# Second edge stage of a graph network: maps turned edge-major, selections moved to ScalarE, values weighted on VectorE

## The chip, the cores and the metric

The kernel runs as one program on one core of a Trainium2 chip. The metric is the device time of one execution in microseconds (us), the median over the executions shown. The engines of the core are TensorE (matrix products, "PE" in the rows, its weight loads "PEld"), VectorE ("DVE"), ScalarE ("ACT"), GpSimd ("POOL") and SyncE ("SP"), which only issues transfers.

## The reference, cut to what matters

Two message-passing layers over a graph of 12,500 nodes and 200,000 edges, sorted by destination. The change touches the edge part of the second layer:

```python
ms = src_s[edge_src] + dst_s[edge_dst]            # 64 scalars per edge
mv = src_v[edge_src] + dst_v[edge_dst]            # 32 vectors of 3 components
o0a = w1 * ms
o0b = w4 * (einsum('eud,ed->eu', mv, Y1) / SQ3)   # Y1: the edge's direction
o1a = (w2 * ms)[:, :, None] * Y1[:, None, :]
o1b = w3[:, :, None] * mv
o1c = w5[:, :, None] * (cross(mv, Y1[:, None, :]) / SQ2)
ls, lv = eq_lin(concat[o0a, o0b], concat[o1a, o1b, o1c], lin_ws, lin_bs, lin_wv)
a = einsum('ehk,hk->eh', smooth_leaky(alpha), alpha_dot)   # 8 heads, alpha = ls[:, :64]
a = exp(a - segment_max(a)); a = a / segment_sum(a)
ns, nv = segment_sum(vs * a), segment_sum(vv * a)          # per destination node
```

## The kernel before, in words

Edges are cut into 1568 tiles of 128 (`ET`, `R`). A step handles four tiles (`GT = 4`), a pass is eight steps (`STEPS = 8`), and the stage `layer1_edges` is 49 passes (`PASSES`). Each engine has its own program: a body of eight unrolled steps, in which `r` is the step in the pass. The first pass and the last are written out, those between are a loop. Order across engines is kept by counting semaphores. Each engine executes in order, so a wait holds all that is queued behind it. `gate` is a wait on a semaphore that has long been set.

The step `i` of the engines, as far as the change touches it:

- SyncE: `load_windows(i+4)` loads for each tile the window of up to 128 destination rows of the table `TD` (`win`, four slots), from starting rows that it reads into registers. Then follow index and weight loads and `store(i, 6)`, which waits for the totals of step `i-6`.
- GpSimd: gathers with indirect transfers, one per tile, the source rows from `TS` and adds them into `m_` (L1952), as soon as ScalarE has put the destination part there. Then `weighted(i, 8)` (L1936) multiplies the 20 values of each head of step `i-8` by the head's exponential.
- VectorE: `sums(i+1)` makes the products with the direction (`prod`), the two halves of the cross product (`cA`, `cB`, L1981 to L1984, each in two pieces as the components wrap around) and their sum and difference; in every fourth step `scans`; `selections(i+4)` (L1970) compares a row of destination ranks with the partition number, which gives the 0/1 matrix `pick`; `results(i-1)` makes logits and values; `weigh(i+1)` multiplies by the edge weights into `d`; `members(i)` (L2018) makes the 0/1 matrix `q` that sums edges per destination.
- TensorE: `spread_out(i+3)` in two halves (L2138) multiplies `pick` with the windows; `turn_back(i-1)` in two halves (L2187) transposes the mapped results to edge-major; `weights(i+1)` (L2124); `turn(i, 0..2)` (L2149) transposes `d`; `totals(i)` in two halves (L2163) sums the values of step `i-6`; `map_scalars(i)` (L2170) and `map_vectors(i)` (L2176, L2177) apply the linear maps with the weights stationary and 512 edges moving, so that the result has channels on partitions; `logits_up` and `tops_down` (L2196, L2201) transpose logits and segment maxima once per four steps.
- ScalarE: copies out of the PSUM banks: `keep_far` (L2266), `keep(i, 0..4)` (L2275), `keep_totals` (L2286), in `results` the hyperbolic tangent and the scalar values (L2295, L2299), and once per four steps `weigh_up` (L2252), the exponential of the logits.

Transposes, windows and maps take turns in PSUM banks 2 and 3, seven uses per step (`bank`). A matrix product in 32-bit floats stands in the trace as two passes, a transpose as one.

## Time and profile before

| | us |
|---|---|
| median of 3 executions | 9799.34 |
| lowest, highest | 9798.74, 9811.15 |
| profiled execution | 9813.87 |
| its span in the trace | 9812.0 |
| TensorE, VectorE, GpSimd, ScalarE busy | 8373.1, 7735.9, 7372.6, 4874.4 |
| second edge stage, first to last gather | 5335.6 to 9015.3 |

The profiled execution is one execution with the recorder on. Its time is 14.5 us above the median. Busy times are means over stages with different limits, so the stage of the change is read by itself. In a timeline row the first number is the start, in us from the span's start, and the second the busy time; a bracket holds the idle time before it and what ended it.

### The profile page before, as it was taken

To read this page: it belongs to the slowest core of one execution; us is meant where nothing else is said; L and a number is where in the kernel's file an instruction comes from. 1 tells how busy PE (TensorE), PEld (TensorE's weight loads), DVE (VectorE), ACT (ScalarE), POOL (GpSimd) and SP (SyncE) were. 2 spreads that over 40 slices of the span, in tenths; PEclk is the share of its full clock that TensorE was granted. 3 is DMA by queue.
4 is the path that set the end of the run, shared out by engine and by line. 5 is a ranking of instruction groups with operands and counts; after the bars stand their busy time and mean duration, and the time that the engine had idled before them with its cause. 6 is when DMAs were issued, how large, how long until landed. Compare 5 with 4: busy or idle time off the path is not lost. (4 is left out here: it accounts for less than half of the span.)

```text
span 9812.0 us, 193495 instructions
## 1 busy us (share of the span) xinstructions
PE 8373.1 (85%) x35878; PEld 5079.2 (52%) x35878; DVE 7735.9 (79%) x14864; ACT 4874.4 (50%) x9073; POOL 7372.6 (75%) x4571
## 2 busy tenths in 40 slices
PE   0788888888888869999985999999999999998588
PEld 0444444444444422222222777777777777777233
DVE  3177777777777768888886999999999999998465
ACT  0176666666666631121121555555555555555355
POOL 4378888888888878778774888888888888886331
PEclk9599999999999989999997999999999999999799
DMA  5578888888888877778773666666666666665222
GB/s 208 180 161 167 167 168 166 167 167 167 167 167 167 167 213 275 267 271 282 264 270 109 136 137 144 137 143 137 144 138 144 138 142 137 144 137 122 59 70 52
DMA packets 1235170, 1618.04 MB, mean 165 GB/s; under 512 B 222610, under 2 KB 1010589, under 8 KB 1178973
## 3 DMA queue, kind: packets, MB, share of 16 engines
q1 hardware_dynamic: 758950, 1273.86, 40.0%
q0 software_dynamic: 475584, 338.58, 27.1%
q14 instruction: 589, 4.83, 0.2%
q8 instruction: 47, 0.77, 0.0%
HBM read 1533.79 MB, written 444.07 MB: 202 GB/s over the span
## 5 line engine op out<-in xcount | busy, mean ns | idle before, releaser
L1952 POOL DMA_INDIRECT e_m<-TS,e_at x1568 | 2631.8, 1678 | 583.7 <-issue 461.4
L442 POOL DMA_INDIRECT sums<-e_total,e_place x1568 | 2506.9, 1599 | 565.9 <-DMA sums<-e_total,e_place 314.5
L579 PE MATMUL ps<-e_win,e_pick 128*128 128x448 f32 x3136 | 1325.8, 568 | 165.0 <-DVE e_u L476 97.0
L579 PEld LDWEIGHTS ps<-e_win,e_pick 128*128 128x128 f32 x3136 | 612.5, 201 | 921.6 <-issue 864.1
L2275 ACT ACTIVATE e_dT<-ps 128x512 f32<-128x512 f32 x1176 | 660.0, 596 | 495.5 <-PE ps L2149 340.1
L2275 ACT ACTIVATE e_oT<-ps 128x512 f32<-128x512 f32 x784 | 468.9, 598 | 615.1 <-PE ps L2177 373.2
L742 DVE SCALAR_TENSOR_TENSOR r_y<-ps,w_rb,r_rstd 128x512 f32<-128x512 f32 x394 | 295.6, 750 | 579.9 <-issue 533.2
L1096 POOL TENSOR_TENSOR n_zv<-n_zv,n_ast 128x1536 f32<-128x1536 f32 x200 | 703.6, 3518 | 36.6 <-DMA n_zv<-in_x_groups 22.5
L1936 POOL TENSOR_TENSOR e_val<-e_val 128x640 f32<-128x640 f32 x392 | 670.9, 1712 | 61.9 <-ACT e_val L2252 61.9
L2018 DVE TENSOR_TENSOR e_q<-e_row,dstI 128x512 f32<-128x512 int32 x392 | 704.2, 1796 | 13.3 <-PE ps L2163 13.3
L711 PE MATMUL ps<-r_sq,w_avg 128*128 128x512 f32 x788 | 458.1, 666 | 277.4 <-issue 277.4
L2124 PE MATMUL ps<-w_r,e_h 128*128 128x224 f32 x3136 | 669.7, 357 | 1.6 <-DVE e_d L2006 1.6
L2138 PE MATMUL ps<-e_win,e_pick 128*128 128x160 f32 x3136 | 592.1, 313 | 83.6 <-DMA e_win<-TD 66.4
L2149 PE MATMUL ps<-ident,e_d 128*128 128x128 f32 x4704 | 641.9, 273 | 3.8 <-ACT e_dT L2275 2.0
L592 PEld LDWEIGHTS ps<-e_u,e_q 128*128 128x128 f32 x3136 | 536.8, 190 | 187.5 <-issue 187.5
L2138 PEld LDWEIGHTS ps<-e_win,e_pick 128*128 128x128 f32 x3136 | 492.9, 198 | 243.9 <-issue 235.1
L620 ACT ACTIVATE e_far<-ps,attr 128x160 f32<-128x160 f32 x1176 | 442.2, 391 | 328.8 <-PE ps L579 209.0
L2163 PEld LDWEIGHTS ps<-e_val,e_q 128*128 128x128 f32 x3136 | 496.4, 192 | 197.1 <-issue 157.9
L2163 PE MATMUL ps<-e_val,e_q 128*128 128x168 f32 x3136 | 585.4, 310 | 7.5 <-ACT e_tot L2286 7.5
L592 PE MATMUL ps<-e_u,e_q 128*128 128x194 f32 x3136 | 580.4, 327 | 0.0
L2124 PEld LDWEIGHTS ps<-w_r,e_h 128*128 128x128 f32 x3136 | 572.1, 193 | 6.0 <-issue 2.0
L2149 PEld LDWEIGHTS ps<-ident,e_d 128*128 128x128 f32 x4704 | 562.2, 141 | 25.0 <-issue 5.3
(448 smaller groups left out, 19299.8 us busy)
## 6 DMA issues: line engine op xcount, KB each, us to landing
e_win<-T SPq DMA_DIRECT2D x1568, 168.0 KB
n_z<-in_x_groups SPq DMA_DIRECT2D x400, 512.0 KB
n_zv<-in_x_groups SPq DMA_DIRECT2D x800, 192.0 KB
TOT<-e_tot SPq DMA_DIRECT2D x392, 352.0 KB, 2.6
e_row<-in_src_rows SPq DMA_DIRECT2D x98, 1024.0 KB
e_local<-LR SPq DMA_DIRECT2D x196, 512.0 KB
e_row<-in_dst_rows SPq DMA_DIRECT2D x98, 1024.0 KB
e_win<-TD SPq DMA_DIRECT2D x1568, 60.0 KB
```

The costliest lines, as they stand in the source:

```text
L442: pool.indirect_dma_start(sums[c], bass.IndirectOffsetOnAxis(ap=place[:, r % 4, c:c + 1], axis=0), total[:, r % 4, c, 0:MSG0], None, compu ...
L579: pe.matmul(g[:, c, :], pick[:, p, R * c:R * c + R], win[:, s, c, :], start=True, stop=True).then_inc(spread, 1)
L592: last = pe.matmul(out[:, c, :], q[:, p, c, :], u[:, p, c, :], start=True, stop=True)
L1096: pool.tensor_tensor(zv[:, b], zv[:, b], ast[:, g.p], ALU.mult).then_inc(zv_ready, 1)
L1936: pool.tensor_tensor(u[:, :, 1:SEG], u[:, :, 1:SEG], bc(u[:, :, 0], SEG - 1, 2), ALU.mult).then_inc(u_ready, 1)
L1952: pool.indirect_dma_start(m_[:, r % 4, c, :], None, TS, bass.IndirectOffsetOnAxis(ap=at[:, gp, col:col + 1], axis=0), compute_op=ALU.add). ...
L2018: dve.tensor_tensor(q[:, j % 2], row[:, gp, R * cols.start:R * cols.stop].rearrange("r (c e) -> r c e", c=GT), bc(dstI[:, 0, bass.ds(i.n(4 ...
L2124: last = pe.matmul(w4[:, c, 0:224], hh[:, p, R * c:R * c + R], W["r3"][:], start=True, stop=True)
L2138: last = pe.matmul(to[:, c % 2], pick[:, p, R * c:R * c + R], win[:, s, c, :], start=True, stop=True)
L2149: last = pe.transpose(ps[:, bank(i, 2 + j), R * c:R * c + R], d[:, p, c, j, :], I[0:R, 0:R])
L2163: last = pe.matmul(tot2[:, c % 2], q[:, j % 2, c, :], val[:, slot // 4, 4 * (slot % 4) + c, :], start=True, stop=True)
L2275: act.activation(to, ps[:, bank(i, 2 + j), :], ACT.Copy).then_inc(kept, 1)
```

## The change

Five things change in `layer1_edges`, and with them the order of several steps:

1. The linear maps take the transposed edges as the stationary operand and the weights as the moving one. The results then lie edge-major in PSUM at once (`scalar_out4` in bank 4, `vector_out4` in bank 5). The two groups of transposes back and two of the five copies by ScalarE per step go. Banks 2 and 3 have five uses per step.
2. The selections move from VectorE (one comparison) to ScalarE (two passes: the absolute distance to the partition number, then the positive part of one minus it).
3. ScalarE repeats two vector components behind the three (`m_` grows by 64 columns), so that each half of the cross product is one VectorE instruction.
4. ScalarE repeats the three direction components per head (`ye`), so that the three products in `results` are one.
5. The weighting of the values moves from GpSimd, eight steps behind, to VectorE, six steps behind, as the first work of a step. `weigh_up` moves from the end of a step `r % 4 == 1` to the next step, behind `keep_far`.

On TensorE `tops_down` stands before the transposes, and the totals stand behind the third transpose and behind the vector map. The core of the diff:

```diff
-        m_ = sb("e1_m", [R, 4, GT, X])
+        m_ = sb("e1_m", [R, 4, GT, X + 2 * V])
-            return 2 + (7 * i.r + j) % 2
+            return 2 + (5 * i.r + j) % 2
...
@@ vector: sums
                     dve.tensor_tensor(prod[:], vec, y[0], ALU.mult)
-                    dve.tensor_tensor(cA[:, :, 0:2], vec[:, :, 1:3], y[2][:, :, 0:2], ALU.mult)
-                    dve.tensor_tensor(cA[:, :, 2], vec[:, :, 0], y[2][:, :, 2], ALU.mult)
-                    dve.tensor_tensor(cB[:, :, 0], vec[:, :, 2], y[1][:, :, 0], ALU.mult)
-                    dve.tensor_tensor(cB[:, :, 1:3], vec[:, :, 0:2], y[1][:, :, 1:3], ALU.mult).then_inc(crossed, 1)
+                    gate(dve, k)
+                    dve.wait_ge(again, i.n(1, 1))
+                    dve.tensor_tensor(cA[:], vec5[:, :, 1:4], y[2], ALU.mult)
+                    dve.tensor_tensor(cB[:], vec5[:, :, 2:5], y[1], ALU.mult).then_inc(crossed, 1)
...
@@ vector: results and weighted
-                    for x in range(3):
-                        last = dve.tensor_tensor(
-                            turn_by_y[:, :, 4 * x:4 * x + 4].rearrange("r (c h) j -> r c h j", c=GT),
-                            vectors4[:, :, :, 12:16], bc(bc(yx[:, x, bass.ds(i.n(4), GT)], HEADS, 2), 4, 3), ALU.mult)
-                    last.then_inc(by_y, 1)
...
+                    dve.wait_ge(mapped, i.n(2, 2))
+                    y3 = ye[:, p].rearrange("r (c h) i -> r (c h) i", c=GT)
+                    dve.tensor_tensor(turn_by_y[:].rearrange("r a (i j) -> r a i j", i=3),
+                                      bc(vector_out4.rearrange("r c (h x) -> r (c h) x", x=16)[:, :, 12:16], 3, 2),
+                                      bc(y3, 4, 3), ALU.mult).then_inc(by_y, 1)
...
+                def weighted(i):
+                    j = i.r - 6
+                    slot, gp = j % STEPS, j % STEPS // 4
+                    gate(dve, k)
+                    dve.wait_ge(exped, i.uses(2, j // 4 + 1))
+                    u = val[:, gp, 4 * (slot % 4):4 * (slot % 4) + 4].rearrange("r c (h x) -> r (c h) x", x=SEG)
+                    dve.tensor_tensor(u[:, :, 1:SEG], u[:, :, 1:SEG], bc(u[:, :, 0], SEG - 1, 2), ALU.mult
+                                      ).then_inc(u_ready, 1)
...
@@ vector: body
+                        if not i.before(6):
+                            weighted(i)
                         if more:
                             sums(after)
...
-                        if i.plus(4).within():
-                            selections(i.plus(4))
...
@@ tensor: maps
-                    pe.matmul(ps[:, bank(i, 5), :], W["la"][:].rearrange("u a h x -> u (a h x)"), dT[:, 0, :], start=True, stop=True
-                              ).then_inc(turned, 1)
+                    pe.wait_ge(kept, i.n(3, 1))
+                    if not i.before(1):
+                        gate(pe, k)
+                        pe.wait_ge(outs, i.n(2))
+                        gate(pe, k)
+                        pe.wait_ge(silued, i.n(2, -1))
+                    for c in range(GT):
+                        last = pe.matmul(scalar_out4[:, c], dT[:, 0, R * c:R * c + R],
+                                         W["la"][:].rearrange("u a h x -> u (a h x)"), start=True, stop=True)
+                    last.then_inc(mapped, 1)
...
+                    for c in range(GT):
+                        pe.matmul(vector_out4[:, c], dT[:, 1, R * c:R * c + R], W["lb"][:].rearrange("u h x -> u (h x)"),
+                                  start=True, stop=False)
+                        last = pe.matmul(vector_out4[:, c], dT[:, 2, R * c:R * c + R],
+                                         W["lc"][:].rearrange("u h x -> u (h x)"), start=False, stop=True)
                     last.then_inc(mapped, 1)
...
@@ tensor: body
+                            spread_out(i.plus(3), 0, far2(i, 0), (far_kept, 5) if i.before(1) else (kept, i.n(3, -1)))
+                            spread_out(i.plus(3), 1, far2(i, 1), (far_kept, 6) if i.before(1) else (kept, i.n(3)))
                         if not (isinstance(t, int) and t == PASSES - 1 and r == STEPS - 1):
                             weights(after)
+                        if r % 4 == 1 and not i.before(5):
+                            tops_down(i)
                         gate(pe, k)
                         pe.wait_ge(d_ready, i.n(1, 1))
                         turn(i, 0)
                         turn(i, 1)
+                        map_scalars(i)
+                        turn(i, 2)
                         if not i.before(6):
                             totals(i, 0)
-                        turn(i, 2)
-                        if r % 4 == 1 and not i.before(5):
-                            tops_down(i)
-                        map_scalars(i)
+                        map_vectors(i)
                         if not i.before(6):
                             totals(i, 1)
-                        map_vectors(i)
...
@@ scalar: selections and body
+                    act.activation(pick[:, p, :], local[:, gp, GT * R * s:GT * R * s + GT * R], ACT.Abs, bias=minus[:, 0:1]
+                                   ).then_inc(distant, 1)
+                    gate(act, k)
+                    act.wait_ge(distant, i.n(1, 1))
+                    act.activation(pick[:, p, :], pick[:, p, :], ACT.Relu, bias=one[:, 0:1], scale=-1.0).then_inc(picked, 1)
...
+                        if r % 4 == 2 and not i.before(6):
+                            weigh_up(i.plus(-1))
+                        if not (isinstance(t, int) and t == PASSES - 1 and r == STEPS - 1):
+                            repeat(At(t, r + 1) if r + 1 < STEPS else At(t + 1, 0))
                         keep(i, 0)
                         keep(i, 1)
+                        if i.plus(4).within():
+                            selections(i.plus(4))
+                        keep(i, 2)
+                        results(i)
```

## Rows read from the trace of the kernel before

**Rows 1.** Busy time per engine in one stretch: PE, PEld, DVE, ACT, POOL, clock, DMA share, GB/s.
```profile
7000.00:7200.00 200.00, 187.21 (x1080) 151.47 (x1079) 191.21 (x453) 114.86 (x245) 171.97 (x107) 1.00 0.62 138
```

**Rows 2.** Timeline of SyncE's queue: stores and last window loads.
```profile
7004.71 0.01 SPq L1873 DMA_DIRECT2D TOT<-e_tot  x1
...
7012.68 0.08 SPq L1851 DMA_DIRECT2D e_win<-TD  x1
...
7033.77 0.43 SPq L1873 DMA_DIRECT2D TOT<-e_tot  x1
...
7039.10 0.08 SPq L1851 DMA_DIRECT2D e_win<-TD  x1
...
7042.29 0.43 SPq L1873 DMA_DIRECT2D TOT<-e_tot  x1
...
7080.01 0.00 SPq L1873 DMA_DIRECT2D TOT<-e_tot  x1
```

**Rows 3.** Timeline of an ordinary step, TensorE and ScalarE.
```profile
7035.65 0.71 PE L2138 MATMUL ps<-e_win,e_pick 128*128 128x160 f32 x4
...
7036.39 0.44 ACT L2266 ACTIVATE e_m<-ps 128x320 f32<-128x320 f32 x1 [0.47 <-PE ps L2138]
...
7036.63 1.68 PE L2124 MATMUL ps<-w_r,e_h 128*128 128x224 f32 x8
...
7038.15 1.04 PE L2149 MATMUL ps<-ident,e_d 128*128 128x128 f32 x8
...
7038.78 1.09 ACT L2275 ACTIVATE e_dT<-ps 128x512 f32<-128x512 f32 x2 [1.27 <-issue]
...
7039.02 0.74 PE L2163 MATMUL ps<-e_val,e_q 128*128 128x168 f32 x4
...
7039.79 0.45 ACT L2286 ACTIVATE e_tot<-ps 128x336 f32<-128x336 f32 x1
...
7040.03 1.02 PE L2170 MATMUL ps<-e_dT,w_la 128*128 128x512 f32 x2
...
7041.46 1.02 PE L2176 MATMUL ps<-e_dT,w_lb 128*128 128x512 f32 x2
...
7043.18 0.71 PE L2138 MATMUL ps<-e_win,e_pick 128*128 128x160 f32 x4
```

**Rows 4.** Timeline of VectorE over two steps.
```profile
7037.97 0.55 DVE L1980 TENSOR_TENSOR e_prod<-e_m,yx 128x384 f32<-128x384 f32 x1
...
7046.84 0.55 DVE L1980 TENSOR_TENSOR e_prod<-e_m,yx 128x384 f32<-128x384 f32 x1
7047.31 0.41 DVE L1981 TENSOR_TENSOR e_cA<-e_m,yx 128x256 f32<-128x256 f32 x1
...
7048.49 0.59 DVE L1987 TENSOR_REDUCE e_dot<-e_prod 128x128 f32<-128x384 f32 x1
...
7049.48 0.47 DVE L1970 TENSOR_SCALAR e_pick<-e_local,nodes_sb 128x512 f32<-128x512 bf16 x1
```

**Rows 5.** Timeline of TensorE: after a wait, and 128-column passes of another stage.
```profile
7015.88 0.41 PE L2196 MATMUL ps<-ident,e_val 128*128 128x128 f32 x1 [2.13 <-issue]
7016.43 0.81 PE L2138 MATMUL ps<-e_win,e_pick 128*128 128x160 f32 x4
...
4409.69 0.39 PE L1368 MATMUL ps<-w_msd,n_ns 65*128 65x128 f32 x2
4409.92 0.49 PE L1369 MATMUL ps<-w_mv,n_yv 96*128 96x192 f32 x2
```

**Rows 6.** The membership test's line: shortest, median and longest duration in ns.
```profile
L2018 DVE TENSOR_TENSOR e_q<-e_row,dstI x392: 680/1941/3000, 5404.7 to 9066.7; 128x512 f32<-128x512 int32 x196
```

**Rows 7.** ScalarE's groups by shape over the whole span: busy us, mean ns.
```profile
L2275 ACT ACTIVATE e_dT<-ps 128x512 f32<-128x512 f32 x1176 | 660.0, 596 | 495.5 <-PE ps L2149 340.1 <-issue 155.4
...
L719 ACT ACTIVATE r_sq<-ps,w_rb 128x512 f32<-128x512 f32 x394 | 270.7, 687 | 138.5 <-PE ps L702 110.5 <-issue 26.8
...
L2252 ACT ACTIVATE e_val<-e_val 128x128 f32<-128x128 f32 x98 | 47.2, 481 | 47.9 <-DVE e_val L2073 41.9 <-issue 5.6
```

More of the change, by code:

```diff
@@ L2100, in _ @@
                 dve.wait_ge(ones_set, 2)
-                for r in range(4):
-                    selections(At(0, r))
                 sums(At(0, 0))
@@ L2109, in _ @@
                 for r in range(5):
+                    weighted(At(PASSES, r))
                     members(At(PASSES, r))
+                weighted(At(PASSES, 5))
             @block.tensor
@@ L2237, in _ @@
                 passes(pe, body)
-                for j in range(2):
-                    turn_back(At(PASSES - 1, STEPS - 1), j)
                 logits_up(At(PASSES, 0))
@@ L2273, in keep @@
                         act.wait_ge(mapped, i.n(2))
-                    to = dT[:, j, :] if j < 3 else oT[:, j - 3, :]
-                    act.activation(to, ps[:, bank(i, 2 + j), :], ACT.Copy).then_inc(kept, 1)
+                    act.activation(dT[:, j, :], ps[:, bank(i, 2 + j), :], ACT.Copy).then_inc(kept, 1)
                 def keep_totals(i, half):
@@ L2324, in _ @@
                         keep_far(At(0, r), half, far2(At(0, 0), half))
+                    if r < 2:
+                        selections(At(0, r + 2))
+                repeat(At(0, 0))
                 passes(act, body)
-                results(At(PASSES - 1, STEPS - 1))
                 weigh_up(At(PASSES, 1))
```

103 lines of the change are left out of this document (41 added, 62 removed).

## The prediction

> **What bounds the kernel now.** The change touches one stage, the second edge stage, 392 steps of four tiles in 49 passes of eight steps. I read first the busy times of a stretch inside it, then the SyncE queue, then the timeline of single steps. VectorE is busy for 191 of 200 us, TensorE for 187, GpSimd for 172, and the granted clock of TensorE is full [rows 1]. ScalarE has room. So three engines are close together, and the busy share doesn't say which of them sets the pace.
>
> The SyncE queue gives the pace, because it issues one store per step behind everything else. An ordinary step takes 8.52 us (7033.77 to 7042.29), and a whole pass 75.30 us (7004.71 to 7080.01), which is 9.41 us per step [rows 2]. So eight ordinary steps would be 68.2 us, and 7.1 us of a pass lie in the steps with the segment scans (two in a pass) and at the loop's edge.
>
> The timeline of an ordinary step shows what the 8.52 us are [rows 3]. TensorE never stops in it: window selection 0.54 twice (0.98 from 7035.65 to 7036.63, less the four transposes back between), edge weights 1.52, twelve transposes at 0.109 (eight in 0.87), totals 0.57 twice (1.01 with four transposes), maps six passes of 0.43 (four in 1.72), eight transposes back 0.87. That is 1.08 + 1.52 + 1.31 + 1.14 + 2.58 + 0.87 = 8.50 us. In ordinary steps TensorE is the bound.
>
> VectorE needs more: from one L1980 to the next 8.87 us [rows 4]. It falls behind by 0.35 us a step, and TensorE pays at the next group border, where it waits for the logits (2.13 us before L2196 [rows 5]) and the maxima. Over a pass the two are equal. The membership test on VectorE takes 0.68 us at its shortest and 1.94 us in the median [rows 6]; which is explained if GpSimd's multiplication of the values, running at the same time, stops it meanwhile.
>
> **The change, part by part.** *VectorE.* The selection goes (0.39 us from one start to the next, 7049.48 having 0.47 busy, 0.08 overlapping). Four cross-product pieces, 1.18 us from 7047.31 to 7048.49, become two of 384 elements, 0.47 and 0.59 as the last must drain: 0.12 less. The three products by direction become one: about 0.12 less. The weighting comes over from GpSimd: 640 elements, from 0.41 for 256 and 0.55 for 384 [rows 4] about 0.83 busy, 0.75 from start to start. The membership test falls to its undisturbed 0.68, 1.27 less. Sum 8.87 - 0.39 - 0.12 - 0.12 + 0.75 - 1.27 = 7.7 us, with the scans (five small instructions per group, some 0.5 us a step) 8.2. GpSimd is busy for 172 of 200 us, 8.1 us of a step of 9.41, and loses the multiplication. Both fall below TensorE's pace, so these savings buy only the 0.35 us per step that TensorE pays at group borders.
>
> *TensorE.* The eight transposes back go, 0.87 us. The maps get 24 passes of 128 columns, each with its own weights, in place of six of 512. The trace has such passes in another stage: two in 0.23 us (4409.69 to 4409.92), 0.115 each [rows 5], while transposes run at 0.109. I take 0.112, so 2.69 us for 2.58. The ends are 0.109 and the 0.135 of the 160-column passes. The engine's own work becomes 8.50 - 0.87 - 2.58 + 2.69 = 7.74 us.
>
> The Trainium skill (TensorE: Matmul & The Clock Gate, Back-to-back issue gap) says that a stream of 128-column matmuls with a weight load each runs at about 81 ns against 56 ns without. On this kernel's passes that ratio would make 0.155 us of 0.107 and add about 1.0 us to a step, an estimate from that page. The row with 0.115 speaks against it.
>
> *New waits of TensorE.* The transposes back and the selections were also what filled the time in which ScalarE empties a bank. Let time run from the first transpose of a step. ScalarE starts its copy at 0.63 (7038.15 to 7038.78), the copy takes 0.60 [rows 7], and TensorE goes on some 0.16 later (the way there takes 0.19, from 0.44 for four transposes to 0.63): 1.39. Before, two groups of transposes (0.87) and the totals (0.57) covered that. Now the scalar map stands directly behind the 0.87: wait 0.52. It ends at 2.4 with a restart of 0.10 (0.81 against 0.71 for the same four passes after a wait, 7016.43 against 7035.65). The third transpose is copied from 3.04 on at the earliest, and not earlier either because ScalarE has two copies (to 1.72) and the two new selection passes ahead (0.69 each, as L719, which also reads a pointer bias [rows 7]). The copy ends at 3.64, the vector map starts at 3.80, and transposes and totals end at 3.42: wait 0.38, restart 0.10. Ordinary step: 7.74 + 0.52 + 0.38 + 0.20 = 8.84 us. It is longer than 8.52 although the engine does 0.76 us less. Ends: 8.58 with no restart and 0.109 per pass, 9.4 with 0.135.
>
> *A new wait per group.* ScalarE takes the exponential of four tiles right behind the copies of the gathered windows in the step r % 4 = 2. VectorE now weights in the same step, as its first work, and queued behind that are the sums, then the first product of the results, which frees the bank that the scalar map of this step writes. From the start of the second window selection: copy starts 0.74 later (7035.65 to 7036.39), takes 0.44, exponential 0.48 [rows 7], release 0.06, weighting 0.75, sums 2.52 (2.64 from 7046.84 to 7049.48, less 0.12), product 0.41, release 0.16: 5.56 us. TensorE would be there after 0.54 + 1.52 + 1.39 = 3.45. Wait 2.1 us, once per four steps. Before, GpSimd weighted two steps later and nobody waited. With the logits' transpose (0.55, 7015.88 to 7016.43) and the maxima's (some 0.1) a group costs 2.8 us.
>
> *At the loop's edge* SyncE takes 7.97 us from a store to the last window load, ordinarily 5.33 [rows 2]. The store waits for the second totals' copy, 1.2 us behind their start (0.77 until it starts, 0.45 long, as for the first half [rows 3]), plus 0.7. So the windows are issued 9.9 us behind the totals, and the selection that needs them comes 8.84 + 0.57 + 0.55 + 0.5 (TensorE's own edge) = 10.5 behind. Landing takes more than nothing and at most 4.1 (7039.10 to 7043.18 gave no wait): a wait of 0 to 3.5 us per pass. I take 0.7, near the lower end, as it is a latency alone.
>
> *Other edits.* The repetition of two components (256 elements, some 0.4 us) and the directions per head cost ScalarE about 0.7 us in idle time; VectorE waits for the first, but has its first product to do. If ScalarE had no room, each 0.1 would delay the copies and TensorE by as much. Prologue and tail change by a few us either way, taken as nothing.
>
> **Sum.** A pass: 8 x 8.84 + 2 x 2.8 + 0.5 + 0.7 = 77.5 us against 75.3, so 49 x 2.2 = 108 us, rounded to 110. The profiled execution took 9813.87 us (span 9812.0), 14.5 above the median of the runs, 9799.34. From the median: 9,910 us.
>
> **Rivals.** *The pace was VectorE's and GpSimd's (faster, large).* If TensorE's waits for ScalarE stay covered and nobody waits for the exponential, 8.2 us of VectorE set the pace: 392 x 1.2 = 475 us less, 9,325 us. For it: 191 of 200 us busy. Against it: ordinary steps already run at 8.5, below VectorE's 8.87. 6 in 100.
>
> *No wait for the exponential (faster, the other side).* One mechanism: the weighting finds the exponential done. Then a pass is 4.2 us shorter, 73.3, 98 us less than before: 9,700; with the lower ends 9,565. It decides where the per-group wait is under 1.0 us. 20 in 100.
>
> *It cancels.* Wait and gain within the measurement's 0.2% (20 us), a step of 9.36 to 9.46: 10 in 100.
>
> *The passes are paced by weight loads, or the windows come late (slower, more).* At 0.135 a pass the step is 9.4, and with 3.5 us per edge 84.9 us per pass: up to 10,260. 12 in 100. (The rule of the TensorE page would give a step of 9.9 and some 10,310, an estimate from that page of the Trainium skill.)
>
> *Forecast*, 9,820 to 10,010: 52 in 100.
>
> **Numbers.** Within 0.2% of before, 20 us, is what a measurement of this kernel can't tell from no change. Slower 0.52 + 0.12 = 0.64, same 0.10, faster 0.26. The range leaves out the first rival, the lower half of the second and the upper half of the last: 9,640 to 10,090.
>
> **What would show it.** In the profile after: ordinary steps at 8.8 (stores on SyncE's queue); TensorE idle some 0.5 us before the scalar map and 0.4 before the vector map, released by ScalarE's copies; once per four steps 2 us before the scalar map, released by VectorE's product; VectorE busy for some 165 of 200 us with waits before the weighting; the membership test at 0.68; map passes at 0.11. I am wrong if ordinary steps are under 8.5, if the scalar map never waits for VectorE, or if VectorE has no idle time left.

## The result and the profile after

The changed kernel takes 10,480.38 us (10,473.55 to 10,496.62, 4 runs), the kernel before 9,799.04 us on the same chip (9,794.77 to 9,811.15). The ratio is 1.0696, 95% interval 1.0677 to 1.0714: 7% slower. The prediction had slower, with 9,910 us and 10,090 us as its upper end.

The busy times of the stretch that stands for the kernel before in [rows 1], now of the changed kernel:

```profile
7000.00:7200.00 200.00, 160.54 (x1079) 149.86 (x1078) 141.65 (x310) 104.16 (x240) 119.48 (x72) 0.93 0.54 121
```

TensorE fell from 187 to 161 us, VectorE from 191 to 142, GpSimd from 172 to 119, the granted clock from 1.00 to 0.93. No engine is near its limit. So the step is a ring of waits and not one engine's work.

SyncE's stores, one a step, as in [rows 2]:

```profile
7500.14 0.44 SPq L1875 DMA_DIRECT2D TOT<-e_tot  x1
7514.40 0.41 SPq L1875 DMA_DIRECT2D TOT<-e_tot  x1
7526.37 0.43 SPq L1875 DMA_DIRECT2D TOT<-e_tot  x1
7535.86 0.42 SPq L1875 DMA_DIRECT2D TOT<-e_tot  x1
...
7615.93 0.43 SPq L1875 DMA_DIRECT2D TOT<-e_tot  x1
```

A pass (7526.37 to 7615.93) takes 89.56 us against 75.30. Over 49 passes that would be 699 us; 681 were measured, so the whole difference lies in this stage. The ordinary step takes 9.49 us (7526.37 to 7535.86) against 8.52, the step with the scans 14.26 us, the one with the exponential 11.97.

Timeline of the ordinary step, all engines (start, duration, engine, line, what it waited for):

```profile
7525.55 1.25 PE L2129 MATMUL ps<-e_win,e_pick 128*128 128x160 f32 x8
...
7526.37 0.90 ACT L2267 ACTIVATE e_m<-ps 128x320 f32<-128x320 f32 x2 [0.17 <-PE ps L2129]
...
7527.17 0.41 ACT L2273 ACTIVATE e_m<-e_m 128x256 f32<-128x256 f32 x1
...
7527.72 0.56 DVE L1961 TENSOR_TENSOR e_cA<-e_m,yx 128x384 f32<-128x384 f32 x1 [3.11 <-ACT e_m L2273]
...
7529.83 0.41 DVE L2006 SCALAR_TENSOR_TENSOR e_silu<-e_silu,ps 128x256 f32<-128x256 f32 x1
...
7530.30 1.16 PE L2167 MATMUL ps<-w_la,e_dT 128*128 128x128 f32 x8 [1.11 <-DVE e_silu L2006]
...
7531.29 0.60 PE L2140 MATMUL ps<-ident,e_d 128*128 128x128 f32 x4
...
7531.73 0.74 PE L2154 MATMUL ps<-e_val,e_q 128*128 128x168 f32 x4
...
7532.58 0.49 PE L2178 MATMUL ps<-w_lb,e_dT 128*128 128x128 f32 x2
...
7534.47 0.74 PE L2154 MATMUL ps<-e_val,e_q 128*128 128x168 f32 x4
...
7535.04 1.25 PE L2129 MATMUL ps<-e_win,e_pick 128*128 128x160 f32 x8
```

Read it as a ring. TensorE selects the new window (7525.55), ScalarE copies it in two parts (7526.37), and only then comes the repetition (7527.17), because it stands behind these copies in ScalarE's queue. VectorE has waited 3.11 us for it. Cross products, sums and the product that frees the scalar maps' bank follow (7529.83), then TensorE's scalar map (7530.30), the rest of its step, and the next window selection (7535.04). The links are 0.82 + 0.80 + 0.55 + 2.11 + 0.47 + 0.99 + 0.44 + 0.85 + 1.89 + 0.57 = 9.49 us. Starts of one chain from a selection to the next add up to the step in any case; that this chain sets the pace shows in the brackets, where ScalarE waited for TensorE, VectorE for ScalarE and TensorE for VectorE, and in the runs below that cut it.

The waits in the stretch 5500 to 9500 us, some 45 passes (us in total, times, longest):

```profile
DVE e_cA L1961 <- ACT e_m L2273: 629.2, 267, 3.3
DVE e_val L2032 <- ACT e_val L2239: 477.3, 89, 6.1
...
PE ps L2167 <- DVE e_silu L2006: 422.6, 267, 2.4
...
PE ps L2195 <- DVE e_top L2055: 218.9, 89, 3.1
...
PE ps L2115 <- DMA e_h<-H: 55.8, 45, 1.5
...
PE ps L2129 <- DMA e_win<-TD: 30.7, 45, 1.1
```

VectorE waits for the repetition and for the exponential; TensorE waits for VectorE's product before the scalar map in three steps of four, and for the maxima once a group.

The first of the two steps with scans in a pass, same timeline:

```profile
7499.43 1.35 PE L2129 MATMUL ps<-e_win,e_pick 128*128 128x160 f32 x8 [1.05 <-DMA e_win<-TD]
7500.35 0.90 ACT L2267 ACTIVATE e_m<-ps 128x320 f32<-128x320 f32 x2 [1.60 <-PE ps L2129]
...
7501.70 0.56 DVE L1961 TENSOR_TENSOR e_cA<-e_m,yx 128x384 f32<-128x384 f32 x1 [3.27 <-ACT e_m L2273]
7502.13 1.78 PE L2115 MATMUL ps<-w_r,e_h 128*128 128x224 f32 x8 [1.34 <-DMA e_h<-H]
...
7505.02 0.42 DVE L2055 TENSOR_TENSOR_SCAN e_top<-e_mask,e_fwd 128x128 f32<-128x128 f32 x1
...
7505.59 0.30 PE L2195 MATMUL ps<-ident,e_top 128*128 128x128 f32 x1 [1.69 <-DVE e_top L2055]
```

And TensorE alone behind it, with the granted clock of 7506 to 7512 (the sixth value, as in [rows 1]):

```profile
7507.50 2.07 PE L2167 MATMUL ps<-w_la,e_dT 128*128 128x128 f32 x8 [0.60 <-ACT e_dT L2281]
...
7519.54 1.16 PE L2167 MATMUL ps<-w_la,e_dT 128*128 128x128 f32 x8 [2.33 <-DVE e_silu L2006]
```

```profile
7506.00:7512.00 6.00, 5.40 (x32) 4.99 (x32) 4.01 (x10) 3.96 (x9) 2.71 (x2) 0.72 0.89 230
```

The transpose of the maxima now stands ahead of the turns, so all of TensorE waits for VectorE's second scan, and that scan is late by the repetition. This step has two more waits, once a pass: 1.05 us for the windows and 1.34 us for the transfer behind them (`e_h`). After these two and the wait for the maxima (1.05, 1.34 and 1.69 us between 7498.4 and 7505.6) the mean of 0.72 says that the clock is at the lower of its two levels, 1.2 GHz, for over half of the 6 us: the same eight passes take 2.07 us instead of 1.16.

### The profile page after: what moved, and what is told of

It reads as the page before. It is cut to its first block and busy times, and to the rows that moved or that the text cites. A ratio compares the mean times of both kernels' runs of the same rounds, so it can differ in the third digit from the quotient of the medians.

```text
span 10471.8 us, 200255 instructions
## 1 busy us (share of the span) xinstructions
PE 8415.0 (80%) x39798; PEld 5558.9 (53%) x39798; DVE 7310.1 (70%) x13298; ACT 5062.0 (48%) x9857; POOL 6851.8 (65%) x4179
## 5 line engine op out<-in xcount | busy, mean ns | idle before, releaser
L579 PEld LDWEIGHTS ps<-e_win,e_pick 128*128 128x128 f32 x3136 | 620.0, 203 | 911.9 <-issue 836.1
L2167 PE MATMUL ps<-w_la,e_dT 128*128 128x128 f32 x3136 | 540.1, 325 | 497.7 <-DVE e_silu L2006 459.3
L2167 PEld LDWEIGHTS ps<-w_la,e_dT 128*128 128x128 f32 x3136 | 459.0, 225 | 587.8 <-DVE e_silu L2006 248.3
L2140 PE MATMUL ps<-ident,e_d 128*128 128x128 f32 x4704 | 733.9, 298 | 0.0
L1961 DVE TENSOR_TENSOR e_cA<-e_m,yx 128x384 f32<-128x384 f32 x392 | 218.2, 557 | 691.5 <-ACT e_m L2273 691.5
L2292 ACT ACTIVATE e_tot<-ps 128x336 f32<-128x336 f32 x784 | 355.0, 453 | 705.8 <-PE ps L2154 484.6
L2178 PE MATMUL ps<-w_lb,e_dT 128*128 128x128 f32 x3136 | 661.0, 294 | 36.7 <-issue 6.2
L2032 DVE TENSOR_TENSOR e_val<-e_val 128x640 f32<-128x640 f32 x392 | 321.3, 820 | 522.6 <-ACT e_val L2239 522.6
L2154 PE MATMUL ps<-e_val,e_q 128*128 128x168 f32 x3136 | 642.5, 332 | 8.9 <-ACT e_tot L2292 7.5
L2180 PE MATMUL ps<-w_lc,e_dT 128*128 128x128 f32 x3136 | 621.0, 281 | 0.0
```

The costliest lines, as they stand in the source:

```text
L579: pe.matmul(g[:, c, :], pick[:, p, R * c:R * c + R], win[:, s, c, :], start=True, stop=True).then_inc(spread, 1)
L2140: last = pe.transpose(ps[:, bank(i, 2 + j), R * c:R * c + R], d[:, p, c, j, :], I[0:R, 0:R])
L2154: last = pe.matmul(tot2[:, c % 2], q[:, j % 2, c, :], val[:, slot // 4, 4 * (slot % 4) + c, :], start=True, stop=True)
L2167: last = pe.matmul(scalar_out4[:, c], dT[:, 0, R * c:R * c + R], W["la"][:].rearrange("u a h x -> u (a h x)"), start=True, stop=True)
L2178: pe.matmul(vector_out4[:, c], dT[:, 1, R * c:R * c + R], W["lb"][:].rearrange("u h x -> u (h x)"), start=True, stop=False)
L2180: last = pe.matmul(vector_out4[:, c], dT[:, 2, R * c:R * c + R], W["lc"][:].rearrange("u h x -> u (h x)"), start=False, stop=True)
```

## The experiments

Ratios are to the kernel before, run on the same chip as each set. Before took 9,836, 9,830, 9,840, 9,848 and 9,837 us in the five sets, so only ratios are compared. The changed kernel's own 1.0696 was measured once, in a set of its own with 9,799 us before, and was not run again beside the others.

Three theories for the 7%. **Queue**: the repetition stands behind ScalarE's copies of the new window, and the two moved steps stretch that chain. **Maps**: 24 passes with the edges stationary, or the clock, cost it. **Selections**: they come late on ScalarE.

**Places in the queues, one at a time.** The first run moves only the repetition:

```diff
+                        if not (isinstance(t, int) and t == PASSES - 1 and r == STEPS - 1):
+                            repeat(At(t, r + 1) if r + 1 < STEPS else At(t + 1, 0))
                         if i.plus(3).within():
                             keep_far(i.plus(3), 0, far2(i, 0))
                             keep_far(i.plus(3), 1, far2(i, 1))
                         if r % 4 == 2 and not i.before(6):
                             weigh_up(i.plus(-1))
-                        if not (isinstance(t, int) and t == PASSES - 1 and r == STEPS - 1):
-                            repeat(At(t, r + 1) if r + 1 < STEPS else At(t + 1, 0))
```

> The changed kernel, with ScalarE's repetition of two vector components put ahead of its copies of the gathered windows, so that VectorE's cross products no longer queue behind TensorE's window selection of the same step. Theory Q (the repetition stands in the wrong place in ScalarE's queue, and sums, scans and the product that frees the scalar map's bank all hang on it): a pass falls from 89.3 us to about 80, ordinary steps from 9.55 to 8.9 us, the wait before the scalar map in ordinary steps goes; 350 to 550 us less than the changed kernel, 9,930 to 10,130. Rival M (the maps with edges stationary cost it: 24 passes with loads, and the lower clock): within 60 us of 10,480. Rival S (the selections on ScalarE come too late): no change either.

Measured 10,167 us, ratio 1.0342 (1.0324 to 1.0359): 313 us less by time, 347 by ratio, just under the 350 expected at least. Half of the loss was the place of one instruction of 0.41 us. VectorE still waits for it (313.7 us in the stretch above, from 629.2), since ahead of it is now the copy of the last step's second totals, which waits for TensorE as well.

The second run puts the transpose of the maxima back behind the third turn, the third takes ScalarE's weighing (exponential and maxima) one step earlier, back to the end of the step r % 4 = 1, and the fourth does all three.

```diff
-                        if r % 4 == 1 and not i.before(5):
-                            tops_down(i)
...
                         turn(i, 2)
+                        if r % 4 == 1 and not i.before(5):
+                            tops_down(i)
```

```diff
-                        if r % 4 == 2 and not i.before(6):
-                            weigh_up(i.plus(-1))
...
                             keep_totals(i, 1)
+                        if r % 4 == 1 and not i.before(5):
+                            weigh_up(i)
```

> The changed kernel, with the transpose of the maxima put back behind the third transpose of a step. Theory Q: the scans still come late, but two transposes and the scalar map no longer wait for all of them, only for the product behind them, so a scan step falls from about 13.7 us by 1 to 2 us, two per pass: 100 to 200 us less, 10,280 to 10,380. If the late scans are no cause in themselves: within 30 us of 10,480. Rivals M and S: no change beyond 30 us.

> The changed kernel, with the exponential of the logits put at the end of ScalarE's step r % 4 = 1 instead of in the next step behind the copies of the windows. Prediction's wait for the exponential (2.1 us per group): a step r % 4 = 2 falls from about 11 us to 9.6, since the queue behind the repetition stays: 100 to 200 us less, 10,280 to 10,380. If the repetition alone sets the chain: under 60 us less. Rivals M and S: no change.

> The three moves together, everything else as in the changed kernel (maps with edges stationary, selections and repetitions on ScalarE, weighting on VectorE). Theory Q with the exponential and the maxima: what is left is TensorE's step with its two waits for ScalarE's copies, 8.8 to 8.9 us, and the loop's edge: a pass of 73 to 75 us, 9,680 to 9,800, so no slower than the kernel before. Rival M: at least 10,200, as the map passes and the lower clock stay.

Measured 1.0446 (1.0429 to 1.0464), 1.0503 (1.0485 to 1.0521) and 1.0203 (1.0186 to 1.0220). The first gave more than expected (2.5%), the second what was expected (1.9%), the three together less: 10,035 us where at most 9,800 was expected. The ordinary step was 8.69 us, so the ring was cut, but a pass was still 79.6 us on average. Something that none of the three edits touch was left.

**Parts of the change, undone or alone.**

```diff
-                    dve.wait_ge(again, i.n(1, 1))
-                    dve.tensor_tensor(cA[:], vec5[:, :, 1:4], y[2], ALU.mult)
-                    dve.tensor_tensor(cB[:], vec5[:, :, 2:5], y[1], ALU.mult)
+                    dve.tensor_tensor(cA[:, :, 0:2], vec[:, :, 1:3], y[2][:, :, 0:2], ALU.mult)
+                    dve.tensor_tensor(cA[:, :, 2], vec[:, :, 0], y[2][:, :, 2], ALU.mult)
+                    dve.tensor_tensor(cB[:, :, 0], vec[:, :, 2], y[1][:, :, 0], ALU.mult)
+                    dve.tensor_tensor(cB[:, :, 1:3], vec[:, :, 0:2], y[1][:, :, 1:3], ALU.mult)
```

> The changed kernel with its third part undone: ScalarE repeats no component, VectorE makes the cross products in the four pieces of before; the edge-major maps, the selections on ScalarE, the weighting on VectorE and the two moved steps stay. Queue theory (VectorE waits each step for a repetition that stands behind ScalarE's copy of TensorE's new window): the waits of VectorE for the repetition are gone, an ordinary step falls from 9.5 to about 8.9 us, the pass from 89.3 to 81-83 us, ratio to the kernel before 1.01-1.035. Map theory (the reversed maps, 24 passes a step, and the lower clock cost the time): the ratio stays 1.06-1.07. Selection theory (VectorE's results wait for the selections on ScalarE): the ratio stays at 1.05-1.07 too.

Measured 1.0286 (1.0269 to 1.0303). The queue theory said 1.01 to 1.035, the two others no change. TensorE's ordinary step was 8.69 us:

```profile
7063.75 1.04 PE L2139 MATMUL ps<-ident,e_d 128*128 128x128 f32 x8
7065.04 1.16 PE L2166 MATMUL ps<-w_la,e_dT 128*128 128x128 f32 x8 [0.25 <-ACT e_dT L2274]
...
7066.47 0.74 PE L2153 MATMUL ps<-e_val,e_q 128*128 128x168 f32 x4
7067.38 0.49 PE L2177 MATMUL ps<-w_lb,e_dT 128*128 128x128 f32 x2 [0.17 <-ACT e_dT L2274]
```

In the step with the exponential TensorE stood idle 2.41 us before the scalar map.

The second of this set puts the selections back on VectorE:

```diff
                             scans(i)
+                        if i.plus(4).within():
+                            selections(i.plus(4))
                         if not i.before(1):
                             results(i.plus(-1))
```

> The changed kernel with the selections back on VectorE, behind the scans. Queue theory: the chain from the repetition to the product that frees the scalar maps' bank is as long or up to 0.4 us longer, so the ratio stays at 1.07 or rises to 1.085. Selection theory: ratio falls to 1.03-1.05. Map theory: no change from 1.07.

Measured 1.1139 (1.1120 to 1.1158). The selection theory is out: their removal from VectorE was a gain. The direction was the queue theory's, the size beyond its 1.085. The ordinary step was 9.9 us, which is the ring of 9.49 plus the one instruction (0.48 busy, 0.40 from start to start); the rest lay in the group steps, at a granted clock of 0.90.

The third leaves the kernel before as it was but for the maps: no transposes back, and

```diff
-                    pe.matmul(ps[:, bank(i, 5), :], W["la"][:].rearrange("u a h x -> u (a h x)"), dT[:, 0, :], ...)
+                    for c in range(GT):
+                        last = pe.matmul(scalar_out4[:, c], dT[:, 0, R * c:R * c + R],
+                                         W["la"][:].rearrange("u a h x -> u (a h x)"), ...)
```

with totals and maps in the changed kernel's order: scalar maps, third turn, first totals, vector maps, second totals.

> The kernel before with the edge-major maps alone (edges as the stationary operand, 24 passes with the weights as the moving one); all else as before. Queue theory: TensorE's own work hardly changes (about 7.7 us a step) and VectorE's step of about 9.4 us stays the pace, so the ratio is 1.00-1.012. Map theory: the reversed maps are what costs; ratio 1.04 or more.

Measured 1.0153 (1.0136 to 1.0170), between the two expectations. VectorE was busy for 385.8 of 400 us there, so it was the pace, and it had become slower: GpSimd's product now fell on other instructions. The cross product's difference, 548 ns before, took 1,631 ns, and the membership test 902 ns against 1,829.

The fourth is the kernel before with the weighting on VectorE and not on GpSimd:

```diff
+                        if not i.before(6):
+                            weighted(i)
                         if more:
                             sums(after)
```

> The kernel before with one part of the change: VectorE and not GpSimd weights the values, as its first instruction of a step. Queue theory, and the rows of before (VectorE's products slowed from 0.68 to 1.94 us beside GpSimd's): VectorE's step falls from 9.4 to about 8.4 us, TensorE's 8.5 us step takes over as the pace; 170-235 us less, ratio 0.975-0.985. If VectorE's extra product costs as much as the slowdown that it ends: ratio 1.00.

Measured 0.9834 (0.9818 to 0.9850): this part alone makes the kernel faster. The ordinary step was 8.51 us. The membership test took 681 ns on average; its rows of 5600 to 7600 us, before and here:

```profile
L2018 DVE TENSOR_TENSOR e_q<-e_row,dstI 128x512 f32<-128x512 int32 x213 | 389.5, 1829 | 0.0
L2004 DVE TENSOR_TENSOR e_q<-e_row,dstI 128x512 f32<-128x512 int32 x222 | 151.2, 681 | 0.0
```

**What was left.** The first run of the next set is the changed kernel with two edits shown above: no repetition, and both moved steps back.

> The changed kernel without the repetition (third part) and with both moved steps back in their old places (the maxima's transpose behind the third turn, the weighing behind the totals' copies, both in steps 1 and 5 of a pass): left are the edge-major maps, the selections on ScalarE, the wide product with the directions and the weighting on VectorE. Queue theory: without the repetition the ordinary step is 8.7 us, and the moved steps are what makes the group steps 10-12.4 us; with both back a pass is 69.5 + 5 to 8 = 75-77.5 us, ratio 1.00-1.02 (additive from the single runs: 1.00-1.015). If the two moved steps cost nothing once nothing waits for a repetition: no change from 1.0286.

The second is the same with ScalarE's selections later:

```diff
-                        if i.plus(4).within():
-                            selections(i.plus(4))
                         keep(i, 2)
                         results(i)
                         if not i.before(6):
                             keep_totals(i, 0)
+                        if i.plus(4).within():
+                            selections(i.plus(4))
+                        if not i.before(6):
                             keep_totals(i, 1)
```

> The same as the run before it, with the two selections of ScalarE put between the copies of the two totals, where ScalarE stood idle 1.65 us in an ordinary step, instead of ahead of its third eviction. Queue theory: TensorE's wait of 0.17 us before the vector maps goes, and results come earlier; ordinary step 8.5, 1.2-2 us less in a pass, ratio 0.98-1.005. If the selections' place is of no weight: the same as the run before it.

The third joins the two single parts, the weighting and the maps:

> The kernel before with the weighting on VectorE and the edge-major maps, nothing else of the change (selections and cross products on VectorE as before). VectorE's step is then some 8.4 us, TensorE's 7.95 plus waits for the two evictions of about 0.5: ordinary step 8.45-8.6, pass 71-75 us, ratio 0.98-1.00 against the 0.983 of the weighting alone. If the reversed maps are what costs: 1.01 or more.

The fourth is the whole change with both moved steps back and the repetition at a new place:

```diff
                         keep(i, 2)
                         results(i)
+                        if i.plus(2).within():
+                            repeat(i.plus(2))
```

> The changed kernel complete, with both moved steps back in their old places, and the repetition kept but for the step after next and behind ScalarE's results, so that it stands behind nothing that waits for TensorE's new window or totals. Queue theory: it is the place in ScalarE's queue and not the repetition's work that costs; VectorE's waits for it vanish and the ratio is that of the kernel without the repetition and the moves, 1.00-1.02. If the work itself costs (ScalarE's busy time, the memory it writes): 1.02-1.035 as with the repetition first in the step.

Measured 1.0169 (1.0147 to 1.0190), 1.0175 (1.0154 to 1.0195), 1.0189 (1.0167 to 1.0211) and 1.0171 (1.0149 to 1.0192). The last says that the repetition's work is free within the 0.2% of the intervals: with it and without it the time is the same once it is issued two steps ahead, although VectorE still waits for it now and then (95 us in 5500 to 8700, against 501.5 in the changed kernel). The place of the selections is of no weight in this arrangement, against my expectation of 1 to 2 us a pass. The third missed: the weighting alone gave 0.983, weighting and maps gave 1.019, although both have ordinary steps of 8.5 to 8.6 us. So the maps bring 3.5% from somewhere. The kernel of the first of the four shows where. SyncE's queue:

```profile
7093.91 0.43 SPq L1875 DMA_DIRECT2D TOT<-e_tot  x1
7099.74 0.35 SPq L1852 DMA_DIRECT2D e_win<-TD  x1
...
7103.08 0.08 SPq L1853 DMA_DIRECT2D e_win<-TD  x1
```

and its TensorE, with the granted clock of 7108 to 7114:

```profile
7092.99 1.25 PE L2128 MATMUL ps<-e_win,e_pick 128*128 128x160 f32 x8
...
7104.57 1.35 PE L2128 MATMUL ps<-e_win,e_pick 128*128 128x160 f32 x8 [2.60 <-DMA e_win<-TD]
7106.76 3.35 PE L2114 MATMUL ps<-w_r,e_h 128*128 128x224 f32 x8 [0.84 <-DMA e_h<-H]
```

```profile
7108.00:7114.00 6.00, 5.81 (x28) 5.10 (x28) 0.00 (x0) 2.53 (x5) 4.90 (x4) 0.60 0.58 115
```

The kernel with the weighting alone, SyncE and TensorE:

```profile
7011.68 0.42 SPq L1873 DMA_DIRECT2D TOT<-e_tot  x1
7017.30 0.35 SPq L1850 DMA_DIRECT2D e_win<-TD  x1
...
7020.67 0.08 SPq L1851 DMA_DIRECT2D e_win<-TD  x1
```

```profile
7012.47 0.71 PE L2138 MATMUL ps<-e_win,e_pick 128*128 128x160 f32 x4
...
7022.06 0.81 PE L2138 MATMUL ps<-e_win,e_pick 128*128 128x160 f32 x4 [0.77 <-DMA e_win<-TD]
```

In both, SyncE takes over 5.6 us from this store to the next window load, and 3.3 more to the last load. This is not at the start of each group, as the expectations below have it, but once a pass, at the loop's edge. Counting the stores from the start of the stage puts the long gap at `r = 0` each time. In all fourteen kernels with the store ahead of the windows, the one before among them, the trace has it 46 times, 4.3 to 6.1 us. That is as often as the loop over passes returns to its start. It is missing at the start of the loop's first pass and of the last pass, which is written out, and all other gaps are 2.8 us at most. With the weighting alone the store is out 0.79 us before TensorE's window selection (7011.68 against 7012.47). With the edge-major maps the second totals stand last in TensorE's step, and their store is out 0.92 us behind it (7093.91 against 7092.99). So the loads are 1.7 us later against TensorE's need: it waits 2.60 us for the windows and 0.84 for the next transfer. Then it falls to the lower clock, where the eight weight passes take 3.35 us instead of 1.68. TensorE's waits for windows in 5500 to 8700 us are 41, one a pass of 79 us. The next set tests this with one edit in SyncE's queue:

```diff
                             load_windows(ahead)
+                        if not i.before(7):
+                            gate(sp, k)
+                            store(i, 7)
...
-                        if not i.before(6):
-                            gate(sp, k)
-                            store(i, 6)
```

> The kernel without the repetition and the moved steps, with SyncE's store of a step's totals put behind the window loads of the next step instead of ahead of them. Window theory: with the edge-major maps the second half of the totals stands last in TensorE's step, its store reaches SyncE's queue some 1.7 us later against TensorE's need, and once a group, where SyncE takes 4.6 to 5.8 us from a store to the next window load, the windows land up to 2.8 us late; the clock then falls for several us. With the loads first these waits go: 4 to 6 us less in a pass, ratio 0.985-1.00 instead of 1.017. If the reversed maps themselves cost it (24 passes, the two waits for ScalarE's evictions): unchanged at 1.01-1.02.

> The kernel before with the weighting on VectorE, and the same edit in SyncE's queue. Window theory: node-major maps have the second totals earlier, so that windows are late by 0.8 us at most there; 0 to 1 us less in a pass, ratio 0.975-0.984 (the weighting alone: 0.983).

> The complete change with all its parts' work, both moved steps back, the repetition two steps ahead and the window loads ahead of the store. By the queue theory and the window theory together nothing of what the change adds stands in the way any more: ratio 0.985-1.00, the same as the run without the repetition. If the repetition's own work counts: 0.5% or more above that run.

> The changed kernel with only SyncE's window loads ahead of the store. In the changed kernel windows are late by 0.7 us once a pass, since TensorE is held up elsewhere (the repetition): the window theory expects little, ratio 1.055-1.07. If the windows are the first cause of the change's loss: 1.05 or below.

Measured 0.9827 (0.9807 to 0.9847), 0.9814 (0.9796 to 0.9832), 0.9831 (0.9813 to 0.9850) and 1.0639 (1.0614 to 1.0664). The first and the third came out slightly below their ranges of 0.985 to 1.00. The same edit is worth 3.4% beside the mended maps, 0.2% (the intervals overlap) beside the maps of before, 0.6% in the changed kernel (by ratio; its time was 10,474 us). The third kernel does all that the changed one does and takes 9,678 us: only the places of four pieces of work in three in-order queues differ between it and 10,480 (the repetition and the weighing on ScalarE, the maxima's transpose on TensorE, the store on SyncE).

Two things bound what this shows. The kernel that joins only the weighting and the maps was not run with this edit; that its 3.5% is the same wait is argued from its trace, where TensorE waits 41 times for windows (63 us in 5500 to 8700). And the complete change with its queues mended, 0.9831, is no faster than the weighting alone, 0.9834, or the weighting with the windows first, 0.9814: in these runs the four other parts together gained nothing.

The stretch 7000 to 7400 us without repetition and moved steps, first with the store ahead of the windows, then with the windows first:

```profile
7000.00:7400.00 400.00, 350.52 (x2443) 321.51 (x2442) 327.51 (x782) 219.74 (x508) 270.08 (x163) 0.97 0.61 134
```

```profile
7000.00:7400.00 400.00, 367.46 (x2675) 343.67 (x2674) 355.52 (x852) 240.81 (x555) 302.49 (x178) 1.00 0.67 145
```

The clock is back at 1.00, and a pass takes 72.4 us instead of 78.8 at this point of the stage. VectorE in the second of them still waits once a group for each of the two steps that were moved back:

```profile
7090.55 0.43 DVE L2061 TENSOR_TENSOR e_val<-e_val,ps 128x128 f32<-128x128 f32 x1 [2.30 <-PE ps L2194]
...
7094.70 0.83 DVE L2031 TENSOR_TENSOR e_val<-e_val 128x640 f32<-128x640 f32 x1 [1.40 <-ACT e_val L2238]
```

The last set goes after these two, and after the wait before the scalar map (0.25 us idle in an ordinary step). The first run has the maxima's transpose ahead of the turns, as the change has it, and

```diff
                         results(i)
+                        if r % 4 == 1 and not i.before(5):
+                            weigh_up(i)
                         if not i.before(6):
                             keep_totals(i, 0)
                             keep_totals(i, 1)
-                        if r % 4 == 1 and not i.before(5):
-                            weigh_up(i)
```

> The kernel with the windows first and without the repetition, and two steps placed anew: the transpose of the maxima ahead of the turns (where the change has it), and ScalarE's weighing behind its results and ahead of the totals' copies of the same step. In the run with the windows first VectorE stood idle 2.30 us for that transpose and 1.40 us for the exponentials, once a group, and TensorE then 1.3 to 1.5 us for VectorE. Theory: the changed kernel's place of the transpose costs only while VectorE hangs on a repetition; here it takes the waits away, 2 to 3 us less in a pass, ratio 0.968-0.976 against 0.983. If VectorE's waits are paid elsewhere anyway: no change from 0.983.

The second also has

```diff
-                        weights(after)
-                        if r % 4 == 1 and not i.before(5):
-                            tops_down(i)
...
                         turn(i, 0)
                         turn(i, 1)
+                        weights(after)
+                        if r % 4 == 1 and not i.before(5):
+                            tops_down(i)
                         map_scalars(i)
```

so that the maxima's transpose goes along and stands behind the first two turns.

> The same, with TensorE's radial weights of the next step (1.5 us) put between the first two turns and the scalar maps, where it waited 0.25-0.4 us for ScalarE's eviction. Theory: the eviction is hidden, ordinary step 8.4 instead of 8.68, 2 us less in a pass, ratio 0.95-0.965. Rival: VectorE gets its weights 1.3 us later each step and becomes the pace; ratio 0.97-0.99.

Measured 0.9747 (0.9727 to 0.9767) and 0.9603 (0.9583 to 0.9623), 9,587 and 9,444 us. TensorE in the second:

```profile
7105.35 1.12 PE L2139 MATMUL ps<-ident,e_d 128*128 128x128 f32 x8
7106.30 1.68 PE L2114 MATMUL ps<-w_r,e_h 128*128 128x224 f32 x8
7107.82 1.05 PE L2166 MATMUL ps<-w_la,e_dT 128*128 128x128 f32 x8
```

No wait before the scalar map, an ordinary step of 8.4 us, a pass of 67.9. It is faster than both kernels, by 4% and by 10% (0.9603 / 1.0696 = 0.898, over two sets). In the first of the two the transpose of the maxima stands where it cost 2.5% in the changed kernel, and it and ScalarE's weighing together gained 0.8%; VectorE's wait for that transpose (174 us in 5500 to 8700) is gone, and TensorE has none for the scans. What each of the two moves gave was not run apart. Nor were these last two edits tried on the kernel with the weighting alone.

## Why the prediction was wrong in size

The sign was right and so was the picture of TensorE's own step. The sum missed 570 of 680 us. By its own steps:

**VectorE's durations: right.** The membership test takes 685 ns in the changed kernel (0.68 expected), the weighting 820 ns (0.83).

**The map passes: right.** 24 passes of 0.112 us and two restarts of 0.10 were 2.89 us; the profile has 0.99 for the eight scalar ones (7530.30 to 7531.29) and 1.89 for the sixteen others (7532.58 to 7534.47), 2.88 us. Only the lower clock made them nearly twice as long (2.07 us against 1.16 for the eight scalar ones). The Trainium skill (TensorE: Matmul & The Clock Gate, Back-to-back issue gap) gives about 81 ns for a 128-column matmul in a stream with a weight load for each, against about 56 ns without, a ratio of 1.45. This trace doesn't show such a ratio: the passes take 0.11 us, as the transposes do, and a quarter of a 512-column pass of before is 0.107.

**New waits of TensorE for ScalarE's copies: right.** 0.52 and 0.38 us were worked out, 8.84 us for the step. Without the repetition the step is 8.69 us: the scalar map starts 1.29 us behind the start of the turns where their own work is 0.88, and the vector map 0.91 behind totals of 0.57 (7063.75 to 7067.38 above), waits of 0.41 and 0.34.

**The wait for the exponential: right in size.** 2.1 us were predicted before the scalar map. The profile has 2.41 without the repetition and 2.33 with it (7519.54 above). The wait behind it:

```profile
7515.19 0.47 ACT L2239 ACTIVATE e_val<-e_val 128x128 f32<-128x128 f32 x1
...
7515.76 0.83 DVE L2032 TENSOR_TENSOR e_val<-e_val 128x640 f32<-128x640 f32 x1 [5.75 <-ACT e_val L2239]
```

**The step that failed** is the sentence "The repetition of two components (256 elements, some 0.4 us) and the directions per head cost ScalarE about 0.7 us in idle time; VectorE waits for the first, but has its first product to do." The duration is right (0.41 us). But I asked only how long the instruction is and not what stands ahead of it in ScalarE's queue. There stand the two copies of the window that TensorE selects in this very step. The rows of before would have given it. From the start of the second selection: 0.74 until its copy starts and 0.44 for it [rows 3], 0.41 for the repetition, 0.06 to release, cross products and sums 2.04, product 0.41 [rows 4], 0.16 to release: 4.26 us. TensorE is there after 3.45. That is 0.8 us in every step, 6.4 us a pass, some 310 us. Moving this one instruction to the start of the step gave back 3.5% (347 us). Its place two steps ahead gave another 0.3%, but those intervals overlap (1.0186 to 1.0220 and 1.0149 to 1.0192).

**The maxima's transpose was mis-sized**: "some 0.1" was its own duration, and it was put down as if it could not wait. It moved past the turns to stand directly behind a scan that the repetition makes late: 1.7 to 3.1 us a group and the clock after it. Both moved steps together were worth 1.4% once the repetition was first in its step.

**The windows at the loop's edge**: place and size were right for the changed kernel. It waits there once a pass, 30.7 us in 45 times, 0.68 us each, where 0.7 was taken. Left out were the wait for the transfer behind the windows (55.8 us in 45 times, 1.24 us each) and what such waits do to the clock. In the changed kernel itself they cost 0.6%, because TensorE is late anyway. Once ScalarE's queue is mended the wait for windows comes to 2.60 us, inside the bound of 0 to 3.5, and costs 3.4%. The rival with late windows held 12 in 100 and went to 10,260; it was the right second mechanism, with no term for the clock.

**The clock** was in no term of the sum. Its mean over the stage went from 0.99 to 0.93, in the stretches behind the long waits.

**What VectorE's savings buy**: 0.35 us a step was predicted, 137 us over the stage. The weighting alone gave 1.66%, 163 us, close to it.

What stays open: what SyncE does in the long gap at the loop's edge, which the kernel before has too (4.5 to 4.6 us, 46 times); how the 570 us that the sum missed divide among the ring, the maxima, the windows and the clock, since the single runs overlap (3.5, 2.5 and 1.9% apart, 4.9% together); and how much of the lower clock's cost belongs to which wait, which no run separates.

## What to carry to other kernels

When work moves to another engine, write down what stands ahead of it in that engine's queue and whether any of that waits for the consumer's own successor: here 0.41 us of work closed a ring of 9.49 us. When the order of one engine's step changes, follow its last product to the queue that stores it, and look at which loads stand behind that store. Undo the parts of a change one by one before the idea is judged, and run the best part alone beside the whole: the complete change, with its queues mended, is 1.7% faster than the kernel before, but so is the weighting alone. With the waits filled a closely related kernel is 4% faster.

## What the runs showed of the hardware

While GpSimd's product ran, some of VectorE's products of two tiles took much longer, and which ones depended on when it ran. The membership test took 1,829 ns on average beside it, 681 ns without. With the maps alone changed, the slow one was another instruction (548 to 1,631 ns). What VectorE loses so was 1.15 us a step before, and some 1.6 us in that kernel. The weighting costs VectorE 0.82 us, less than GpSimd's weighting cost it.

TensorE fell to the lower clock behind idle times of 2.60 and 0.84 us close together (the kernel without the repetition and with the moved steps back), and the mean granted clock of 7108 to 7114 was 0.60. For 3.4 us of waiting it so paid another 2.5 us: 1.67 for the weight passes (3.35 against 1.68) and 0.87 for the eight transposes (1.91 against 1.04). Together that is 6.0 of the 6.4 us by which a pass at this point grew shorter with the windows first.

In a loop of 47 passes SyncE's gap from a store to the next window load was 4.3 to 6.1 us at each of the 46 returns of the loop, and at most 2.8 us elsewhere.
